# Value products joined two groups to a bank in a pipelined attention kernel

## What is computed

```python
q = (side + b_self) @ Wq + bq          # 8 x 256 x 256, split in 16 heads
k = concat([x + b_prev, side + b_self]) @ Wk + bk
v = concat([x, side]) @ Wv + bv
score_prev = (q . k_prev) / 4          # keys past seq_len masked
score_self = (q * k_self).sum(-1) / 4
weights = softmax(concat([score_prev, score_self]))
x1 = x + (weights[..., :-1] @ v_prev + weights[..., -1:] * v_self) @ Wo + bo
# second layer
s = tanh(x1 @ W1 + b1) @ v             # one score for each row
p = softmax(masked s)                  # prefix, postfix or all but itself
out = x1 + (p @ x1) / count
```

## Time and profile before

| | |
|---|---|
| median of 3 runs | 283.82 us (282.74 to 286.48) |
| the profiled execution | 282.1 us, its span 280.4 us |
| instructions | 5862; TensorE 2004 matmul records, ScalarE 289, VectorE 382 |
| mean granted clock of TensorE over the span | 0.926 of full |
| value products (L1042) | 512 records, 35.6 us busy |
| copies of value products (L525) | 32, 12.3 us busy |

### The profile page before, as it was taken

One profiled execution on the slowest core, in us unless ns is written; L12 is line 12 of the kernel. 1 busy time (PEld: TensorE's weight loads), 2 busy tenths in 40 slices (PEclk: granted clock), 3 DMA queues, 4 the chain that ended last, 5 costly groups with the idle time before them and its releaser, 6 DMA issues.

```text
span 280.4 us, 5862 instructions
## 1 busy us (share of the span) xinstructions
PE 237.1 (85%) x2004; PEld 178.1 (63%) x2004; DVE 180.4 (64%) x382; ACT 153.9 (55%) x289; POOL 65.9 (23%) x79
## 2 busy tenths in 40 slices
PE   2965977997999999999999999999997779675542
PEld 2855755765867786778677767786775547444422
DVE  2873767575686778778877787788677447324231
ACT  4422426755866586658665866586656443770220
POOL 8060100301150135013401440333043004304101
PEclk9979899999999999999999999999999757999555
DMA  5499479259436933593469346724651010201001
GB/s 152 102 300 228 121 246 239 79 188 205 108 112 182 197 119 118 174 219 103 141 187 188 105 148 184 145 79 149 180 124 43 0 42 0 77 2 37 0 0 37
DMA packets 28020, 35.48 MB, mean 127 GB/s; under 512 B 4440, under 2 KB 24416, under 8 KB 28000
## 3 DMA queue, kind: packets, MB, share of 16 engines
q1 hardware_dynamic: 27360, 33.12, 44.2%
q0 software_dynamic: 640, 2.10, 2.1%
HBM read 20.26 MB, written 14.69 MB: 125 GB/s over the span
## 4 chain that ended last, share of the span: by engine, by line
PE 68%; DVE 13%; issue 6%; ACT 4%; DMA 4%; SPq 2%; POOL 1%; DVEq 0%; ACTq 0%; POOLq 0%
PE ps_any L981 15%; PE ps_any L1042 12%; PE ps_max L1016 10%; PE ps_any L996 8%; PE ps_any L988 5%; PE ps_exp L1029 5%; PE ps_any L1203 4%; DVE s_max L783 4%; PE ps_any L1142 3%; PE ps_any L1101 2%; PE ps_any L1073 2%; PE ps_any L1150 2%; DVE x1t_lo L866 2%; DVE pool_pt_lo L932 2%; ACT pool_pt_hi L621 2%
## 5 line engine op out<-in xcount | busy, mean ns | idle before, releaser
L783 DVE TENSOR_REDUCE s_max<-ps_max 128x4 f32<-128x1024 f32 x64 | 78.1, 1220 | 30.7 <-PE ps_max L1016 30.6
L518 ACT ACTIVATE pt<-ps_exp 128x1024 f32<-128x1024 f32 x64 | 65.6, 1025 | 54.8 <-PE ps_exp L1029 54.5
L1016 PE MATMUL ps_max<-k_rows,q_rows 49*128 49x256 f32 x256 | 33.8, 341 | 8.7 <-DVE s_max L783 5.8
L1042 PE MATMUL ps_any<-pt,v_aug 128*32 128x256 f32 x512 | 35.6, 398 | 1.2 <-ACT pt L518 1.2
L475 POOL TENSOR_TENSOR attn<-num,rden 128x256 f32<-128x256 f32 x16 | 9.6, 622 | 111.9 <-DVE rden L922 111.9
L1016 PEld LDWEIGHTS ps_max<-k_rows,q_rows 49*128 49x128 f32 x256 | 20.4, 193 | 21.6 <-issue 13.4
L1029 PE MATMUL ps_exp<-q_rows,k_rows 51*128 51x256 f32 x256 | 27.6, 290 | 0.0
L981 PE MATMUL ps_any<-w_hi,xst_hi 128*128 128x256 f32 x64 | 21.5, 336 | 4.2 <-DVE prod L887 4.2
L1029 PEld LDWEIGHTS ps_exp<-q_rows,k_rows 51*128 51x128 f32 x256 | 21.0, 193 | 0.8 <-issue 0.5
L1042 PEld LDWEIGHTS ps_any<-pt,v_aug 128*32 128x32 f32 x512 | 13.8, 112 | 12.0 <-issue 3.8
L452 POOL TENSOR_TENSOR vs_p<-v_self,p_self 128x256 f32<-128x256 f32 x16 | 9.6, 614 | 40.6 <-ACT p_self L581 40.6
(11 more groups left out here) (133 smaller groups left out, 544.6 us busy)
## 6 DMA issues: line engine op xcount, KB each, us to landing
q_rows<-q_spill SPq DMA_DIRECT2D x32, 192.0 KB, 4.2
k_rows<-k_spill SPq DMA_DIRECT2D x32, 192.0 KB
q_spill<-q_hi SPq DMA_DIRECT2D x16, 256.0 KB, 2.5
k_spill<-k_hi SPq DMA_DIRECT2D x16, 256.0 KB, 2.5
s_sb<-in_fside_BxSxS SPq DMA_DIRECT2D x8, 256.0 KB, 5.7
x_sb<-in_x SPq DMA_DIRECT2D x8, 256.0 KB, 5.4
q_spill<-q_lo SPq DMA_DIRECT2D x8, 256.0 KB, 2.1
k_spill<-k_lo SPq DMA_DIRECT2D x8, 256.0 KB, 2.7
```

The lines of the kernel that those rows point to most:

```text
L518: nc.scalar.activation(pt[:, at:at + 2], ps_exp[:], ACT.Exp).then_inc(p_ready, 1)
L783: nc.vector.tensor_reduce(s_max[:, j // MJ, :, :, j % MJ].rearrange("p t e -> p e t"), ps_max[:], AX.X, ALU.max).then_inc(max_found, 1)
L1016: last = pe.matmul(ps_max[:, e, t], q_rows[par][rows, j, P * t:P * t + P], k_rows[par][rows, j, :], start=True, stop=True)
L1042: last = pe.matmul(bank[32 * c:32 * c + 32, 0, :], v_aug[par][:, t, h, :], pt[:, h % 8, t, :], start=(t == 0), stop=(t == KB - 1), skip_gr ...
```

## The change

Two groups, eight heads, now run back to back into one whole bank (one group to each half), with one increment of pv_ready and one copy of 128x512 to o_sb. They stand at slots 4 and 12, and their copies at slots 5 and 13; nothing of them is left in slots 0 and 8. There are two steps PV0 and PV1 in SHARED, both in bank 3. pt has 16 heads in place of 8, so an exponential waits only for the value products that read the same heads a batch earlier.

```diff
 SHARED = [
-    ("TS", 1, 1, ("st_lo", 1)), ("PV0", -1, 2, ("pv_copied", 1)),
+    ("TS", 1, 1, ("st_lo", 1)),
...
-    ("PV1", -1, 3, ("pv_copied", 2)),
+    ("PV0", -1, 3, ("pv_copied", 1)),
...
-    ("PV2", -1, 3, ("pv_copied", 3)),
...
-    ("PV3", -1, 3, ("pv_copied", 4)), ("PT", -2, 0, ("pt_lo", 1)),
+    ("PV1", -1, 3, ("pv_copied", 2)), ("PT", -2, 0, ("pt_lo", 1)),
...
-    PG = GRP // 2
+    NV = 2
+    VG = NG // NV
...
-        pt = sb("pt", [P, 2 * GRP, KB, S])
+        pt = sb("pt", [P, H, KB, S])
...
             def exps(i, k, j):
                 act.wait_ge(scored, count(i, k, NJ, j + 1))
-                if (n := count(i, k, NG, j // PG - 1)) is not None:
+                if (n := count(i, k, NV, j // (NJ // NV) + 1 - NV)) is not None:
                     act.wait_ge(pv_ready, n)
-                at = 2 * j % (2 * GRP)
-                nc.scalar.activation(pt[:, at:at + 2], ps_exp[:], ACT.Exp).then_inc(p_ready, 1)
+                nc.scalar.activation(pt[:, 2 * j:2 * j + 2], ps_exp[:], ACT.Exp).then_inc(p_ready, 1)

             def pv_copy(i, k, g):
-                act.wait_ge(pv_ready, count(i, k, NG, g + 1))
+                act.wait_ge(pv_ready, count(i, k, NV, g + 1))
...
-                nc.scalar.activation(o_sb[:, g], ps_any[:, bank_free(f"PV{g}", i, k)[0], 0, :], ACT.Copy).then_inc(pv_copied, 1)
+                nc.scalar.activation(o_sb[:, VG * g:VG * g + VG], ps_any[:, bank_free(f"PV{g}", i, k)[0]], ACT.Copy
+                                     ).then_inc(pv_copied, 1)
...
-                    g = {1: 0, 5: 1, 9: 2, 13: 3}.get(s)
+                    g = {5: 0, 13: 1}.get(s)
...
             def pv(i, k, g, pi, pk):
-                pe.wait_ge(p_ready, count(i, k, NJ, PG * (g + 1)))
+                pe.wait_ge(p_ready, count(i, k, NJ, NJ // NV * (g + 1)))
...
-                for t in range(KB):
-                    for c in range(GRP):
-                        h = GRP * g + c
-                        last = pe.matmul(bank[32 * c:32 * c + 32, 0, :], v_aug[par][:, t, h, :],
-                                         pt[:, h % 8, t, :], start=(t == 0), stop=(t == KB - 1),
-                                         skip_group_check=True)
+                for half in range(VG):
+                    for t in range(KB):
+                        for c in range(GRP):
+                            h = GRP * (VG * g + half) + c
+                            last = pe.matmul(bank[32 * c:32 * c + 32, half, :], v_aug[par][:, t, h, :],
+                                             pt[:, h, t, :], start=(t == 0), stop=(t == KB - 1),
+                                             skip_group_check=True)
...
-                    if s % 4 == 0 and live(*prv):
-                        pv(*prv, s // 4, i, k)
+                    if s in (4, 12) and live(*prv):
+                        pv(*prv, s // 8, i, k)
```

More of the change, by code:

```diff
@@ L52 @@
 BANKS = 4
-PER_BATCH = {"mt_copied": 2, "num_done": 2, "masked_done": 2, "pv_copied": 4}
+PER_BATCH = {"mt_copied": 2, "num_done": 2, "masked_done": 2, "pv_copied": 2}
 def build(nc, x, side, seq_len, kind, Wq, bq, Wk, bk, Wv, bv, Wo, bo, b_prev, b_self, W1, b1, v, out):
@@ L635, in period @@
                         act.wait_ge(v_ready, count(*nxt, 1, 1))
-                        if (n := count(*nxt, NG, -NG)) is not None:
+                        if (n := count(*nxt, NV, -NV)) is not None:
                             act.wait_ge(pv_ready, n)
@@ L1098, in period @@
                             bank = take_bank(f"NAT{t}", i, k)
-                            pe.wait_ge(pv_copied, count(*prv, NG, NG))
+                            pe.wait_ge(pv_copied, count(*prv, NV, NV))
                             for gg in range(NG):
```

## The result

| | before | after |
|---|---|---|
| median | 283.86 us (282.74 to 286.48, 4 runs) | 293.97 us (293.04 to 295.72, 4 runs) |
| ratio, 95% interval | 1 | 1.0385 (1.0343 to 1.0427) |
| profiled execution, span | 282.1, 280.4 | 293.04, 291.3 |
| granted clock over the span | 0.926 | 0.900 |

The forecast was 287.3, so the direction was right and 6.7 us of the size are missing.

The account below looks back on a forecast made before the run. TensorE was taken to bound the middle, sharing a tight hand-over with VectorE. Period terms 0.7 - 0.2 + 1.0 + 0.7 + 1.3 gave +3.5 us on the 283.8 median: 287.3 us, range 282.5 to 291.0.

Parts of the forecast that it names:

- A group of value products: On TensorE, a second group joined on adds 0.86 us of streaming, making a joined pair 1.86 us.
- Slots 0 to 2: Slot 2's maximum pair waits for VectorE's slot-0 maximum, starting at +2.58 us; gain 0.92, not 1.10.
- SB: Product after slot 8 in a steady period: 0.46 of the 1.00 us removed becomes a wait for prod.
- pool_pt_lo: Behind slot 12's joined group, the chain moves as a whole; TensorE's wait for it stays 0.26 us.
- Steady period: Periods 3 to 6: -0.06 - 0.54 + 0.86 = +0.26 us each, 27.8 to 27.9 long; four add +1.0.
- Period 1: No older batch; removing slot 8's group gains nothing because VS waits for prod; about +0.7 us.
- Period 2: No o_out in slot 0 and longer between prod and SB; -0.2 us.
- Period 7: No next batch; slot 8's gain goes into a VectorE wait; about +0.7 us, ends -0.5 and +1.7.
- Period 8: Last period: +0.86 us for the last group behind the last exponential, +0.5 for the x1t chain; +1.3.
- that rival: Longer idle in period 8 brings half clock from 236 to 252 us, up to 6.9 us more; chance 0.15.
- The buffer and the copies: 16-head exponential buffer priced at 0; wider copy to o_sb priced at 0, up to 0.1 us.
- theory A: Experiments' theory, whole run: order costs some 3.5 us; the loss beyond it is half clock at start and ends.

Follow-up runs that it names:

- e_first: Changed kernel's plan with only the first two groups joined, at slot 4; third and fourth alone at slots 8 and 12; 288.25 us, 1.0154 of the kernel before.
- filled pair: f_before and f_after: the kernel before and the changed kernel, both with unused dummy matmuls ahead of TensorE's long waits; medians differ by 10.8 us.
- e_ends: Changed kernel, but batches 0 and 7 have four separate groups at slots 0, 4, 8, 12 as before; 286.33 us, 1.0167 of the kernel before.
- e_ends4: Changed kernel, but batches 0, 1, 6 and 7 have four separate groups as before; 287.48 us, 1.0159 of the kernel before.
- e_tail: Changed kernel, but only the last batch (7) has four separate groups as before; 294.36 us, 1.0307 of the kernel before.
- e_four: Kernel before with only the buffer of 16 heads added, its four groups left at slots 0, 4, 8, 12; 286.25 us, ratio 0.9947.
- e_head: Changed kernel, but only batch 0 has four separate groups as before; 290.86 us, 1.0274 of the kernel before.
- c_after: The changed kernel repeated without edits; 297.53 us, 1.0465 of the kernel before.
- e_last: Changed kernel, but the first two groups stand apart at slots 0 and 4, only the second pair joined at slot 12; 292.12 us, 1.0322 of the kernel before.
- e_slot8: Changed kernel with the first joined pair at slot 8 in place of slot 4; 292.61 us, 1.0185 of the kernel before.
- c_before: The kernel before repeated unchanged for a second profile; 282.46 us, one execution.
- f_before: Kernel before plus unused dummy matmuls ahead of TensorE's long waits in the first and last periods; 292.99 us, 1.0319 of the kernel before.
- f_after: Changed kernel plus unused dummy matmuls ahead of TensorE's long waits in the first and last periods; 303.75 us, 1.0536 of the kernel before.

## Why the prediction was right about the order and wrong about the size

- *A group of value products.* Predicted 0.86 for each group joined on, 1.86 in all, 1.9 in the timeline. Measured 164.94 - 163.08 = 1.86, and 1.93. The rule of the Trainium skill on weight loads (TensorE: Matmul & The Clock Gate, Part 3), taken strictly, would have had 2.00; the same part exempts loads into a background weight buffer. The trace disagrees with the strict rule for these tiles, with 1.86.
- *Slots 0 to 2.* Predicted: the slot-2 pair at +2.58, bound by the maximum. Measured 158.69 - 156.12 = 2.57, 0.06 behind the end of that maximum at +2.51.
- *SB.* Predicted a wait of 0.46 for prod, measured 0.36.
- *pool_pt_lo.* Predicted unchanged at 0.26, measured 0.27.
- *Steady period.* Predicted 27.85, measured 27.84; the joined second pair at slot 12 is what costs, since e_first, without it, has 27.5 to 27.7.
- *Period 1.* Predicted +0.7. +0.6 at a like clock, and by the estimate above about 24.6 for 24.5 without the half clock; measured in the profiled execution +1.9.
- *Period 2.* Predicted -0.2, measured -0.1.
- *Period 7.* Predicted +0.7 (-0.5 to +1.7); measured -1.4 in the profiled execution and -0.5 in the filled pair. The sign was wrong, and the value stood at the wrong end of its bounds. The profiled executions also differ in clock there, 10.2 us at half after and 13.6 before.
- *Period 8.* Predicted +1.3. At full clock it is +1.6. Measured +6.9. **This is the step that failed.** The sum took the clock of the kernel before for the changed one, and so had nothing for the 11.6 us at half clock in period 8. The clock stood in the prediction as a rival, with a chance of 0.15, and that rival had the stretch right and the size nearly: half of 6.9, or 3.5. Only its reason was off, since the wait for the last exponential didn't grow; the new waits are at slot 0. In the stretch up to pool_p the two kernels differ by 6.5; e_ends, e_ends4 and e_tail, with the old order there, come within 1.0 of the kernel before, and that 1.0 is the late start of its period 8. What is left, 5.6 against them, is 1.6 for the order and by difference 4.0 for the clock.
- *The buffer and the copies.* Priced at 0; e_four is 0.9947 (0.9873 to 1.002).

Two terms were in the forecast with no such size, +1.5 in period 0 and +1.5 in period 6 (a steady one, +0.26). The first goes with the clock: period 0 has no value products in any of these kernels, and takes 18.5 to 23.9 us in them (18.5 in e_head with period 0 at full clock, 23.9 in e_four with it at 0.67; 3.4 us at half before, 6.8 after). The second is a single collision of the profiled execution (below), and c_after has 28.0 there.

Over all executions the clock can be weighed roughly. In the 32 of the kernel before that ran beside the experiments, the time rises by 0.29 us for each us at half clock (the half-clock time worked out from each execution's span and mean granted clock as 2 x span x (1 - clock); correlation 0.90). They average 286.6 us with 45.3 us of it, the ten of the changed kernel 296.2 with 59.5. So of 9.6 us some 14 x 0.29 = 4 go with the clock. The other 5.5 are more than the 3.2 of the filled pair (0.8 in period 1 and 0.1 in period 2, both counted without half of their half clock, 1.2 - 0.5 + 1.6 in the rest). Where the 2 us between lie is not settled, so for the whole run theory A is shown only in part. The half clock ahead of the clock's record is in none of these figures, and half clock in a stretch where TensorE sets the pace costs more than the mean price, 4.0 us for the 11.6 us in period 8.

Also open in part is what lets the clock fall. All five profiles of kernels whose last batch had its second pair joined (after, c_after, e_head, e_last, e_slot8) had 8 to 12 us of half clock in period 8 before the transposes of pool_p. Of the six unfilled ones with four groups there (before, c_before, e_tail, e_ends, e_ends4, e_four), five had none and e_four had 3.4; e_first, joined at slot 4 only, had 6.8. Each is one profile. For the fall at +2.9 the pair of e_head and e_ends shows what comes before it, a missing group of slot 0 and a TensorE that works 1.33 us in place of 2.32. It is not the only way: e_last and e_ends run alike for the first 4.6 us of period 8, with 2.96 and 2.95 us of work, and the clock falls in the one at +4.6 and not in the other. What differs there lies ahead of period 8, and no run took period 7 apart.

## What to carry to other kernels

When work is taken out of a place where an engine is about to wait, the time does not come back, it becomes idle time; when it is put behind the last producer of a chain, all of it is paid. A walk of the order priced that well here, to 0.1 us in a steady period. It does not price the first and last periods, where TensorE has waits and its clock is not granted in full: there, take the other clock level as a case of its own with a real chance, and compare stretches with the same records at the same granted clock before blaming an order.

## What the runs showed of the hardware that was not expected

- **The same program, other clocks.** c_before and the kernel before fall to half clock at the same places, to 0.4 us. But the kernel before took 281.12 to 292.86 us over 32 executions, with granted clocks of 0.955 to 0.888. A single pair of profiles can't tell 3% of order from 3% of clock.
- **Half clock can be cheap.** From period 8's transposes of pool_p on, the granted clock is 0.61 to 0.79 in the twelve unfilled profiles, and that stretch takes 27.8 to 29.9 us. The two go together (27.8 at 0.79 in e_slot8, 29.4 at 0.73 in c_after, 29.8 at 0.61 in after; correlation 0.84), but a us at half clock costs 0.13 us there, against 4.0 / 11.6 = 0.34 in the stretch ahead of it.
- **The mean granted clock leaves out the beginning.** The record of the clock begins 9.4 to 19.5 us into the span, and what it misses shows above in the windows of f_before and f_after. In seven of the fourteen profiles (e_first, e_four, e_slot8, e_head, e_ends, e_ends4, f_after) the first 128x512 products come at 13.4 us and are 0.43 us apart for most or all of them; in the other seven they come at 11.6 to 12.8, 0.24 apart.
- **A tiny VectorE operation slowed eightfold beside GpSimd.** In period 6 of the changed kernel, VectorE's neg_max took 1.31 us in place of 0.17:

```profile
183.94 0.17 DVE L790 TENSOR_TENSOR t_max<-s_max,s_self 128x16 f32<-128x16 f32 x1
184.15 1.31 DVE L795 TENSOR_SCALAR neg_max<-t_max 128x16 fp32r<-128x16 f32 x1
185.49 0.17 DVE L798 SCALAR_TENSOR_TENSOR neg_max<-t_max,neg_max 128x16 fp32r<-128x16 f32 x1
...
184.14 1.28 POOL L485 TENSOR_TENSOR x_bo<-xr_sb,bias_out 128x512 f32<-128x512 f32 x1 [0.22 <-DMA xr_sb<-in_x]
...
185.72 0.39 PE L1052 MATMUL ps_any<-ident,neg_max 128*16 128x128 f32 x2 [0.43 <-DVE neg_max L798]
186.59 0.66 PE L996 MATMUL ps_any<-ident,attn 128*128 128x128 f32 x4 [0.49 <-DVE o_out L954]
```

It lies beside GpSimd's addition x_bo, begins with it and ends with it, and TensorE waited 0.92 us for what came of it. When x_bo begins depends on when a DMA lands (0.22 us idle before it), so the collision comes in one execution and not in another: in c_after x_bo begins 1.22 us behind neg_max, which takes 0.17 there, and TensorE has no such wait. At the start of period 8 the same befalls t_max, with 1.15 to 1.18 us, in the kernel before as in all the others. The Trainium skill (SBUF — State Buffer, SBUF: two separate sides) has a port pair that VectorE and GpSimd share as an exclusive lock, held for a whole instruction; the trace agrees, with 1.31 for 0.17 beside an x_bo of 1.28. The section names VectorE operations with two inputs in SBUF or in a mode that uses both ports; t_max has two inputs, neg_max has one, and no run here shows its mode.
